# Row maxima of the attention scores: whole-array matmuls with both parts of the queries, in place of pairs in the array's row halves

## The reference

```python
qkv = jnp.einsum('bchw,oc->bohw', x, w_qkv)
q, k, v = jnp.split(qkv, 3, axis=1)             # each reshaped to (b, 8, 64, 1024); q * SCALE
sim = jnp.einsum('bhdi,bhdj->bhij', q, k)
attn = jax.nn.softmax(sim, axis=-1)
out = jnp.einsum('bhij,bhdj->bhid', attn, v)
out = out.transpose(0, 1, 3, 2).reshape(b, HEADS * HEAD_DIM, H, W)
y = jnp.einsum('bchw,oc->bohw', out, w_out) + b_out[None, :, None, None]
mean_sq = jnp.mean(y * y, axis=1, keepdims=True)
y = y * jax.lax.rsqrt(mean_sq + SCALE) * rms_scale[None, :, None, None]
return y + x
```

## Time and profile before

| what | us |
|---|---|
| median of 3 runs | 4198.86 |
| the profiled execution | 4197.25 |
| its span in the profile | 4195.5 |
| TensorE matmuls busy | 4085.2 (97%) |
| TensorE weight loads busy (beside the matmuls) | 2399.6 (57%) |
| VectorE busy | 2860.5 (68%) |
| ScalarE busy | 2272.3 (54%) |
| GpSimd busy | 2856.0 (68%) |

### The profile page before, as it was taken

The page is one execution under the profiler, slowest core; times in us unless marked ns, Lnnn a source line. Parts: engine busy times, 40 slices in busy tenths (PEclk is TensorE's granted clock), DMA queues, the critical chain, the costliest instruction groups (busy, mean ns, idle before and its releaser), DMA issues.

```text
span 4195.5 us, 53061 instructions
## 1 busy us (share of the span) xinstructions
PE 4085.2 (97%) x18624; PEld 2399.6 (57%) x18624; DVE 2860.5 (68%) x2684; ACT 2272.3 (54%) x3969; POOL 2856.0 (68%) x2204
## 2 busy tenths in 40 slices
PE   7999999999999999999999999999999999999996
PEld 5555555555555555555555555555555555555553
DVE  5667666677666767666676766767667666677765
ACT  3556555565555555555555555645556555455553
POOL 4667676676666767767676676767667676676666
PEclk8999999999999999999999999999999999999998
DMA  3101111111111111111011010111111111111100
GB/s 142 41 32 60 51 41 61 51 45 47 51 60 41 51 41 63 48 41 71 21 66 55 31 71 31 61 51 38 63 50 41 51 41 61 51 51 41 61 21 31
DMA packets 71270, 212.19 MB, mean 51 GB/s; under 512 B 8152, under 2 KB 8280, under 8 KB 58208
## 3 DMA queue, kind: packets, MB, share of 16 engines
q1 hardware_dynamic: 71008, 208.80, 13.9%
HBM read 168.92 MB, written 39.85 MB: 50 GB/s over the span
## 4 chain that ended last, share of the span: by engine, by line
PE 68%; issue 12%; POOL 8%; DVE 6%; ACT 6%; DMA 0%; POOLq 0%; ACTq 0%; DVEq 0%
PE aux L442 15%; PE pv L587 14%; PE score L572 9%; PE aux L499 8%; PE aux L475 7%; PE score L574 7%; PE aux L553 6%; POOL prob_sum L975 4%; DVE maxima L831 2%; ACT probs L656 2%; POOL prob_sum L971 1%; ACT q_hm L665 1%; ACT q_hl L663 1%; ACT q_hl L681 1%; POOL x_lo L285 1%
## 5 line engine op out<-in xcount | busy, mean ns | idle before, releaser
L975 POOL TENSOR_TENSOR prob_sum<-prob_sum,probs 128x512 f32<-128x512 f32 x1536 | 1977.0, 1311 | 459.6 <-ACT probs L656 457.2
L831 DVE TENSOR_REDUCE maxima<-aux 128x1 fp32r<-128x1024 f32 x1024 | 1205.8, 1219 | 891.5 <-PE aux L553 820.5
L656 ACT ACTIVATE probs<-score 128x512 f32<-128x512 f32 x2048 | 1110.6, 594 | 947.5 <-PE score L574 939.9
L587 PE MATMUL pv<-probs,v_sb 128*64 128x512 f32 x4096 | 991.8, 605 | 0.0
L572 PE MATMUL score<-q_hl,k_hh 128*128 128x512 f32 x2048 | 881.6, 430 | 9.9 <-ACT probs L656 8.2
L574 PE MATMUL score<-q_hm,k_l 72*128 72x512 f32 x2048 | 816.7, 399 | 0.0
L971 POOL TENSOR_TENSOR prob_sum<-probs 128x512 f32<-128x512 f32 x256 | 344.6, 1367 | 661.5 <-ACT probs L656 661.5
L442 PE MATMUL aux<-x_hi,w_ring 128*128 128x512 f32 x2048 | 669.6, 408 | 20.0 <-DVE x_lo L285 11.1
L572 PEld LDWEIGHTS score<-q_hl,k_hh 128*128 128x128 f32 x2048 | 387.4, 189 | 276.9 <-issue 174.9
L587 PEld LDWEIGHTS pv<-probs,v_sb 128*64 128x64 f32 x4096 | 248.1, 136 | 482.7 <-issue 431.6
L442 PEld LDWEIGHTS aux<-x_hi,w_ring 128*128 128x128 f32 x2048 | 358.9, 189 | 178.1 <-issue 69.4
(11 more groups left out here) (74 smaller groups left out, 4422.4 us busy)
## 6 DMA issues: line engine op xcount, KB each, us to landing
w_ring<-w_split SPq DMA_DIRECT2D x93, 1024.0 KB, 4.8
x_stage<-x SPq DMA_DIRECT2D x128, 256.0 KB, 4.6
resid<-x SPq DMA_DIRECT2D x128, 256.0 KB, 5.8
out<-resid SPq DMA_DIRECT2D x128, 256.0 KB, 2.0
w_split<-w_ring SPq DMA_DIRECT2D x3, 1024.0 KB, 11.6
w_split<-y_sb SPq DMA_DIRECT2D x3, 1024.0 KB, 3.8
y_sb<-wqkv SPq DMA_DIRECT2D x4, 512.0 KB, 7.9
probs<-wqkv SPq DMA_DIRECT2D x2, 512.0 KB, 7.2
```

Of the source, the lines that this page charges most:

```text
L587: pe.matmul(pv[half][e * D:(e + 1) * D, :], v_sb[:, pair // 2, j, (pair % 2) * P + e * D:(pair % 2) * P + (e + 1) * D], probs[:, j % 4, e, ...
L656: act.activation(probs[:, j % 4, e, :], score[e][:], ACT.Exp, scale=SOFT).then_inc(prob_ready, 1)
L831: dve.tensor_reduce(maxima[:, n:n + 1], bank(k, 2), AX_X, ALU.max).then_inc(aux_free[k], 1)
L975: pool.tensor_tensor(prob_sum[:, e, :], prob_sum[:, e, :], probs[:, j % 4, e, :], ALU.add).then_inc(prob_added, 1)
```

## The change

In the common form, the two matmuls of a head take all 128 rows of `q_hl` (low and high part of the queries) against all 128 rows of `k_hh`, where before each took the 64 rows of a high part in its own row half. The waits, banks, reductions and the early form stay.

```diff
@@ -546,12 +546,12 @@
                     pe.wait_ge(q_repeated, 2 * (body.b * SLOTS + slot + 2))
                     if nhalf == 0:
                         pe.wait_ge(k_repeated, 4 * (body.b * PAIRS + (slot + 1) // 2 + 1))
+                cols = slice(it * P, (it + 1) * P)
                 for e in range(2):
                     k = claim(body, slot, f"M{it}{e}", two=True)
                     for h in range(2):
-                        rows = slice(h * D, (h + 1) * D)
-                        last = pe.matmul(bank(k + h), q_hi_at(nhalf, e, h, it),
-                                         k_hh[rows, npair % 2, e, h * HALF:(h + 1) * HALF],
+                        last = pe.matmul(bank(k + h), q_hl[:, nhalf, e, cols],
+                                         k_hh[:, npair % 2, e, h * HALF:(h + 1) * HALF],
                                          start=True, stop=True)
                     last.then_inc(aux_full[k], 1)
```

## The result

The changed kernel takes 4302.08 us (median of 4, 4300.62 to 4302.86), the one before 4198.72 in the same comparison: 1.0246 times as long, 95% interval 1.0229 to 1.0264, so 103.4 us more. The forecast was 4292, between 4268 and 4327.

The account below looks back on a forecast made before the run. TensorE sets the pace, waiting about 0.1 us for VectorE in an ordinary block. 3.68 + 2.00 + 0.27 + 0.03 gives 5.98 us a batch, 95.7 in 16, minus 0.7: 4197 + 95 = 4292 us, range 4268 to 4327.

Parts of the forecast that it names:

- The bound: TensorE, busy 97% of the span, sets the pace, but waits about 0.1 us for VectorE in an ordinary block.
- TensorE's own price: Lost overlap in the maxima matmuls, less one saved array switch, costs TensorE alone 0.26 to 0.27 us a block.
- The ordinary block: In 16 blocks a batch, VectorE's later first reduction delays the following projection item: 0.23 us each, 3.68 a batch.
- The query projection: Eight blocks a batch followed by this projection: 0.25 us each, midway between reduction (0.23) and TensorE's stream (0.27), 2.00 together.
- Slot 5's first block: One block a batch with no item behind it; the next score matmul waits for an exponential, so all 0.27 us is paid.
- The three blocks with a cover: Three blocks whose item is held longer by GpSimd or VectorE's queue (0.28, 0.77, 0.34 us): the change priced at nothing.
- rival B: VectorE falls behind in slots 1, 2 and 5: up to 0.23 us at three blocks, 11 in all, 4303 us; chance 0.10.
- early blocks: Three blocks of 32 in a batch (L539), unchanged, where head 0's banks already fill after the second pair: priced at nothing.
- A: TensorE's whole cost comes through: 29 blocks a batch pay 0.27 us, 125 in all, giving 4322 us; chance 0.13.
- C: Another engine's late work hides the whole change: price 0, time 4197 us, within 8; chance 0.04 together with E.
- D: A block's whole-array matmuls step at 0.12 us instead of 0.23: 0.12 a block, 46 in all, 4243 us; chance 0.03.
- E: The 1844 maxima matmuls still overlap two at a time, so time ends near 4197 us; chance 0.04 together with C.

Follow-up runs that it names:

- order-only kernel: Kernel before, overlap in row halves kept, but both heads' matmuls for the first 512 keys precede those for the second in all blocks: 4306.77 us.
- short reductions: Both kernels with VectorE reducing only the first 512 of 1024 keys: 4090.84 us for the kernel before, 4187.94 for the changed one.

## Why the prediction was right, and where its terms were off

**The bound.** That TensorE sets the pace but waits for head 0's first reduction before an ordinary item was right; the order-only kernel shows it, since it leaves TensorE's stream as it was, moves that reduction's start, and loses all that the change loses.

**TensorE's own price**, 0.26 to 0.27 a block: right as a number (0.26 with short reductions), and right in not being the price of a block with an item behind it.

**The ordinary block**, 16 x 0.23: the block distances grew by 0.19 to 0.28, 0.23 on average.

**The query projection**, 8 x 0.25: each grew by 0.21 to 0.24. It hangs on the reduction like the others, for it grew as much with the order alone changed: 1.79 instead of 2.00 a batch.

**Slot 5's first block**, 0.27: measured 0.21, and nothing in the order-only kernel, so it is TensorE's stream, as forecast.

**The three blocks with a cover.** Two were priced right or a little too high: they soaked up 0.04 and 0.12 of earlier losses, within my bound. The third, slot 2's third block, was priced at nothing, and the block's own change does cost nothing (all but slot 2's second block changed). The 0.24 behind it comes from the second block, for it is there with that one alone changed: its cover, VectorE's queue, moved with what happened before it. That such a cover was "set going before the block" did not make it independent of the change.

**What the sum lacked** is one term, slot 2's second block: 0.77 us a batch behind it and the 0.24 behind the next, 1.01 together, 15 us in the 15 batches that have this scaling. I took that block for ordinary because VectorE came to its reduction in time. But VectorE was full from there to the next block, and one of its instructions stood within some hundredths of a microsecond of a GpSimd instruction. This is the place of my rival B, and not its mechanism: B let a lag grow by the delay itself, up to 0.23 a block; what happened is that a delay of 0.23 changed who came first, for 1.02. With the terms as measured: 3.70 + 1.79 + 0.21 + 0.03 - 0.16 + 0.24 + 0.77 + 0.03 in the early blocks gives 6.61 a batch by these medians; times 16, less 0.7 in the last slot, 0.8 in the first batch, which has no scaling of y there, and 1.0 by which the changed kernel is ahead when the first batch begins (not explained), 103.3 us against the 103.4 of the medians and the 103.3 between the two spans.

**The rivals.** A is ruled out by the order-only kernel; C by all of it; D by the steps, which are 0.23; E by the page's row and by the first score matmul at 1.04. The time lies within the range and even within the forecast's own bounds (4275 to 4312), but that is partly luck: their top rests on 0.25 a block and on 12 us for covers that might go. Neither came about, and the 15 us came from a meeting that no term and no rival had; smaller misses the other way, of about 0.4 us a batch, took up part of them.

## What to carry to other kernels

Before asking what a change does to the engine that is busiest, ask which finished piece the next step waits for, and when that piece is finished: here the order of four matmuls was worth as much as their overlap. A place in the trace that already does what the change does everywhere (the early blocks) is better evidence than a sum of durations. Where two engines share something and their instructions start nearly together, price both outcomes, however small the shift.

## What the runs showed of the hardware that I had not expected

- A scaling with two SBUF operands on VectorE takes 0.77 us ahead of a GpSimd addition and 1.79 behind its start, in all of 15 batches each way.
- Beside a row of GpSimd additions two joins of two columns with their operands in SBUF, 0.3 us elsewhere, took up to 3.46 us, longer than one or two additions of 1.27.
- TensorE's waits of 0.70 us before a block and 1.01 us behind it were followed by a granted clock of 0.50 in 4 of 15 batches, and a single block's change so cost 1.4 to 1.6 us more in such a batch; with 0.67 and 0.56 it was so in 2 of 15, with 0.70 and 0.74 in none.
- Being released by a semaphore costs TensorE 0.11 us beyond the wait, the weight load that is not hidden; the next step shows it (0.34 instead of 0.23).
